# A graph network with a mixture of experts: the router's logits with the gate as standing operand, node numbers on three engines, and four groups

## The chip, the core and the metric

The kernel runs on one core of a Trainium2 chip. A core has TensorE (matrix products, into PSUM), VectorE, ScalarE and GpSimd, each with its own in-order queue, and SyncE, which only issues DMAs; they order their work by semaphores. The metric is the time of the device in microseconds, the median over runs.

## The reference

There are 6250 nodes with 256 features and 200000 edges sorted by destination. What is computed:

```
xn = layernorm(x)
x  = x + relu(GCN(xn)) + mix(xn)       # edges: gather, scale, sum by destination; mix: linear attention and MLP
h  = layernorm(x)                      # "x2" is this x
logits = h @ gate_w + gate_b           # 8 experts
idx = argmax(softmax(logits)); prb = its probability
pos = number of earlier nodes with the same idx
kept = pos < C                         # C = ceil(1.25 * 6250 / 8) = 977
y[n] = expert idx[n] (h[n]) * prb[n] * kept[n]     # 256 -> 1024 relu -> 256
out = x + nan_to_num(y)
```

An expert works on its kept nodes in the order of their numbers, at places 0 to 976. So the router has to turn the idx of each node into a list of node numbers by expert and place.

## The kernel before

Nodes lie in 49 blocks of 128 (a node is a partition of its block). Three stages follow each other: `prepare`, `aggregate_and_mix` (the edges, gathered by GpSimd's indirect DMAs, with the mix beside them) and `tail`. The tail is the router, some 95 us, and then the eight experts. Only the router and what touches its buffers is changed.

The router works in groups of blocks, given by RB (L64): 12, 12, 12, 8 and 5 blocks. All its order is written out by hand, in each engine's own program; within it:

- VectorE (loop at L1681 and behind) sums each block's x2 (L1456, tile acc), takes its statistics (L1461, stt), and after a group aggregates them (L1466, mvg). Between the blocks of a group it does the steps of the group before, at places that `steps` gives (of 24 gaps): `normal` (the root's input veps, the reciprocal inv, one Newton step, the columns of res for the feature table), `choose` (logits lg from PSUM, maximum, ex, candidate, one-hot oh), `counted`, `probability`, `assign`. `chain` lets an instruction raise the semaphore dv and `chained` waits for all that were chained so far, statistics too. In `assign` the place within the expert becomes a slot number; its upper part gives the one-hot one_hi (expert and row of 128, 64 columns), its lower 7 bits one_lo (128 columns), and two products with kept_lo and kept_hi put the node's number, in two parts, on one_hi (node_of, L1581 and L1584). In the second group four instructions low_w1 (L1613) for the first expert's weights stand between the blocks.
- TensorE takes blocks by pairs t: `turn` transposes a pair by four instructions (L1838, e_t), ScalarE copies it to xT_r (L1728), `logits` then multiplies with the pair's features as the standing operand and the 8 gate columns as the moving one (L1849): two products per block, each in two instructions for float32, so the logits come out with a node per partition. `places` counts the nodes before (L1863 to L1871), in the middle of the next group; `owners` (L1881) adds one_lo transposed times node_of over all blocks in p_map, after the last logits of the next group.
- ScalarE, per pair: copy, `scale` of two blocks (L1744, what goes to the feature table). Once a group a root (L1733), in front of the group's last copy, and an exponent (L1738); each of the two needs its own table, so a table load stands before each.
- SyncE sends for each group the feature rows (L1346) once its columns are there and the x2 rows (L1352); the load of w1 for the next expert (L1335) waits for the last low_w1.
- GpSimd makes constants at the start and then waits until slots_ok is 2 (slot_node is written, L1714) and all ten DMAs of the router have landed; then it gathers the first expert's rows (L1389).

## Time and profile before

| | us |
|---|---|
| median of 3 runs | 2598.12 (2594.09 to 2600.07) |
| the profiled execution's own time | 2596.97 |
| its span, first to last instruction | 2595.3 |
| TensorE busy, matrix instructions | 1927.2 |
| GpSimd busy | 1793.1 |
| VectorE busy | 1245.3 |
| ScalarE busy | 797.4 |
| mean granted TensorE clock | 0.874 |

The profile is of one execution. Its page has the busy time of each engine, the span in 40 slices, the chain of work that ended last and the costliest groups of instructions; the trace behind it can be asked for single stretches. PE is TensorE (PEld its weight loads), DVE is VectorE, ACT is ScalarE, POOL is GpSimd, SPq is SyncE's queue. A granted clock of 1.00 is 2.4 GHz, 0.50 is 1.2 GHz. L and a number is the line of the kernel.

### The profile page before, as it was taken

What the parts mean: (1) busy time and instruction counts of PE and PEld (TensorE: products, weight loads), DVE (VectorE), ACT (ScalarE), POOL (GpSimd) and SP (SyncE); (2) the same over time, 40 slices, a digit from 0 to 9 for tenths busy, and PEclk for the clock granted to TensorE, in tenths of its full rate; (3) what the DMA queues carried; (4) which work ended last, traced back from release to release, by engine and by line L of the source; (5) the groups of instructions that cost most, each with busy time, mean ns of one, the idle gap of its engine ahead of it and who ended that gap; (6) DMA issues with size and microseconds to landing.
All of it is one profiled execution on the core that took longest, in us unless ns stands there. A gap on an engine that the chain in (4) does not pass through costs nothing. (4 is left out here: it accounts for less than half of the span.)

```text
span 2595.3 us, 33207 instructions
## 1 busy us (share of the span) xinstructions
PE 1927.2 (74%) x8866; PEld 1534.0 (59%) x8866; DVE 1245.3 (48%) x3250; ACT 797.4 (31%) x1559; POOL 1793.1 (69%) x1908
## 2 busy tenths in 40 slices
PE   8588887666776766776777777766666676999997
PEld 6355555455555555655555555655444575888886
DVE  6334323344444453443544444443322385878886
ACT  5222222133333333332333333332000054444442
POOL 6577777777777777777777777777777602666665
PEclk9799999899888898888888888888877756999998
DMA  7433333333333333333333333333333444222220
GB/s 223 129 104 106 106 106 106 105 105 105 105 106 104 106 104 106 106 105 105 105 106 105 105 106 106 104 105 106 105 105 105 131 147 117 63 79 67 86 70 8
DMA packets 128069, 270.88 MB, mean 104 GB/s; under 512 B 33608, under 2 KB 71460, under 8 KB 127770
## 3 DMA queue, kind: packets, MB, share of 16 engines
q0 software_dynamic: 82992, 221.52, 29.9%
q1 hardware_dynamic: 44906, 47.32, 5.6%
q8 instruction: 77, 1.26, 0.2%
q14 instruction: 94, 0.77, 0.1%
HBM read 244.15 MB, written 27.35 MB: 105 GB/s over the span
## 5 line engine op out<-in xcount | busy, mean ns | idle before, releaser
L776 POOL DMA_INDIRECT ring<-node_rows,src_chunk x1563 | 1484.7, 950 | 493.1 <-issue 475.8
L800 PE MATMUL p_item<-ring,sel 128*128 x3512 | 1018.0, 434 | 536.8 <-SPq L757 534.3
L800 PEld LDWEIGHTS p_item<-ring,sel 128*128 128x128 f32 x3512 | 708.0, 214 | 774.7 <-issue 684.0
L1063 DVE TENSOR_TENSOR acc<-acc,p_item 128x256 f32 (+1 forms) x439 | 184.2, 419 | 826.7 <-PE p_item L800 822.4
L1045 DVE SCALAR_TENSOR_TENSOR sel<-dst_chunk,nbase,p_col 128x512 f32<-128x512 f32 x439 | 326.7, 744 | 57.1 <-issue 38.8
L1934 PE MATMUL e_y<-w2h,hTh 128*128 128x256 f32 x512 | 150.8, 295 | 3.6 <-DVE hTl L1643 3.6
L1389 POOL DMA_INDIRECT rows<-node_features,slot_row x64 | 72.3, 1130 | 114.5 <-DMA out_dram<-res 95.4
L1934 PE MATMUL e_y<-w2h,hTl 128*128 128x256 f32 x512 | 145.4, 284 | 0.0
L1934 PE MATMUL e_y<-w2l,hTh 128*128 128x256 f32 x512 | 145.3, 284 | 0.0
L957 ACT ACTIVATE x1T<-p_t,col_ln1b,col_ln1g 128x128 f32<-128x128 f32 x98 | 39.5, 453 | 343.9 <-PE p_t L833 343.9
L1141 DVE SCALAR_TENSOR_TENSOR kf<-p_q,ke 128x256 f32<-128x256 f32 x49 | 20.8, 425 | 203.7 <-ACT ke L940 203.7
L964 ACT ACTIVATE gT<-p_t,col_b 128x128 f32<-128x128 f32 x98 | 30.7, 364 | 266.8 <-PE p_t L841 266.8
L1921 PE MATMUL e_f<-bTh,w1h 128*128 128x490 f32 (+1 forms) x256 | 101.7, 397 | 11.8 <-ACT hbuf L1777 11.1
L1415 POOL TENSOR_TENSOR low<-low,big 128x256 f32<-128x256 f32 x64 | 51.8, 809 | 81.1 <-DVE big L1657 80.5
L1934 PEld LDWEIGHTS e_y<-w2h,hTh 128*128 128x128 f32 x512 | 98.6, 192 | 5.2 <-DVE hTl L1643 5.2
L1921 PE MATMUL e_f<-bTl,w1h 128*128 128x490 f32 (+1 forms) x256 | 100.3, 392 | 0.0
L1777 ACT ACTIVATE hbuf<-e_f,fb_sb 128x490 f32<-128x490 f32 (+1 forms) x128 | 80.0, 667 | 65.4 <-DVE hTl L1643 38.5
L1921 PE MATMUL e_f<-bTh,w1l 128*128 128x490 f32 (+1 forms) x256 | 99.4, 388 | 0.0
L1934 PEld LDWEIGHTS e_y<-w2l,hTh 128*128 128x128 f32 x512 | 98.8, 193 | 0.0
L1934 PEld LDWEIGHTS e_y<-w2h,hTl 128*128 128x128 f32 x512 | 98.5, 192 | 0.0
L869 PE MATMUL p_q<-wq_sb,xnT_m 128*128 128x512 f32 x196 | 97.5, 622 | 0.0
L1406 POOL DMA_INDIRECT out_dram<-oo,slot_node x64 | 79.1, 1236 | 26.5 <-DVE oo L1634 15.4
(257 smaller groups left out, 2921.9 us busy)
## 6 DMA issues: line engine op xcount, KB each, us to landing
ring<-node_rows,src_chunk POOLq DMA_INDIRECT x1563, 2.7
w1raw<-in_w SPq DMA_DIRECT2D x8, 1024.0 KB, 5.0
w2raw<-in_w SPq DMA_DIRECT2D x8, 1024.0 KB, 6.7
res<-in_x SPq DMA_DIRECT2D x7, 896.0 KB, 9.9
node_features<-res SPq DMA_DIRECT2D x3, 1554.0 KB, 7.5
out_dram<-res SPq DMA_DIRECT2D x3, 1536.0 KB, 10.6
node_rows<-acc SPq DMA_DIRECT2D x4, 1024.0 KB, 4.9
node_rows<-acc SPq DMA_DIRECT2D x3, 512.0 KB, 5.0
```

The costliest lines, as they stand in the source:

```text
L776: nc.gpsimd.indirect_dma_start(ring[:, c % RING // U, c % U, :], None, table, bass.IndirectOffsetOnAxis(src_chunk[:, c:c + 1], 0)).then_in ...
L800: mm = pe.matmul(p_item[bank(i)][:, 0:C], sel[:, i % SELR, u, :], rows[:, u, :], start=(u == 0), stop=(u == U - 1), skip_group_check=True)
L869: mm = pe.matmul(p_kv, xnT[:, a, :], wq_sb[:, a, C:3 * C], start=(a == 0), stop=(a == CH - 1))
L957: nc.scalar.activation(x1T[:, a, :], p_t[:, a, :], ACT.Identity, scale=g["cols"]["ln1g"][:, a:a + 1], bias=g["cols"]["ln1b"][:, a:a + 1]). ...
L1045: nc.vector.scalar_tensor_tensor(sel[:, i % SELR, :, :], dst.rearrange("p (u e) -> p u e", e=1).broadcast_to([P, U, P]), nbase[:, bass.ds( ...
L1063: nc.vector.tensor_tensor(a, a, p_item[bank(j)][:, 0:C], ALU.add).then_inc(added, 1)
L1389: nc.gpsimd.indirect_dma_start(rows[0:r, e % 2, t, :], None, feats, bass.IndirectOffsetOnAxis(slot_row[0:r, k:k + 1], 0)).then_inc((gather ...
L1406: nc.gpsimd.indirect_dma_start(out, bass.IndirectOffsetOnAxis(slot_node[0:r, k:k + 1], 0), oo[0:r, t % 2, :], None, bounds_check=N - 1, oo ...
L1415: nc.gpsimd.tensor_tensor(low[0:r, t % 2, :], low[0:r, t % 2, :], big[0:r, t % 2, :], ALU.add).then_inc(pool_st, 1)
L1777: nc.scalar.activation(hbuf[:, j % 2, h * NH[0]:h * NH[0] + NH[h]], p_f[(2 * j + h) % 4][:, 0:NH[h]], ACT.Relu, bias=fb1_sb[:, bass.ds(e, ...
L1921: mm = pe.matmul(p_f[c % 4][:, 0:NH[h]], w[:, a, j * P:(j + 1) * P], b[:, a, h * NH[0]:h * NH[0] + NH[h]], start=(q == 0), stop=(q == len( ...
L1934: mm = pe.matmul(p_y[t % 2][:, 0:C], h[:, j, t * P:(t + 1) * P], w[:, j, :], start=(q == 0), stop=(q == len(parts) - 1))
```

## The change

RB gives four groups of 14, 14, 14 and 7 blocks. The gate weights become the standing operand: one product for both blocks of a pair gives 8 partitions of up to 256 nodes, ScalarE copies these to lgT, and TensorE transposes them back to the bank that `choose` reads. node_of is no longer made by two products of VectorE: ScalarE makes the low part (a scaled copy with node_lo as the scale), GpSimd the high part, but VectorE for the last group. kept_lo and kept_hi are gone: the place is limited to RT * P - 1 = 1023, the last slot of an expert, which lies behind the 977 kept ones. The statistics raise bn_ok instead of dv. `owners` of a group comes one pair into the second group after it. The steps of VectorE stand at other places; low_w1 of the first expert stands behind the slots; ScalarE's root comes in front of the next group's first copy, in the last group in front of its last scale. one_lo and node_of share the memory of rows. The semaphores of the edges' dst rows are used again as arrived.

```diff
-RB = [0, 12, 24, 36, 44, NBLK]
-RGM = 12
+RB = [0, 14, 28, 42, NBLK]
+RGM = 14
...
GpSimd
-            nc.gpsimd.iota(e8[:], [[1, EXP]], EXP, 0, allow_small_or_imprecise_dtypes=True).then_inc(const3, 1)
+            nc.gpsimd.iota(e8[:], [[RT * P, EXP]], EXP * RT * P, 0, allow_small_or_imprecise_dtypes=True).then_inc(const3, 1)
...
+            pool.wait_ge(const3, 9)
+            for gi in range(NG - 1):
+                q, k = gi % 2, size(gi)
+                pool.wait_ge(one_hi_ok, gi + 1)
+                wait(pool, mapped, gi - 1)
+                nc.gpsimd.tensor_tensor(node_of[:, q, 0:k, 1, :], one_hi[:, q, 0:k, :],
+                                        node_hi[:, blocks(gi)].rearrange("p (b e) -> p b e", e=1)
+                                        .broadcast_to([P, k, NS]), ALU.mult).then_inc(high_node, 1)
             pool.wait_ge(slots_ok, 2)
             pool.wait_ge(dma_out, 16 * NOUT)
...
VectorE
-                chain(V.bn_stats(stt[:, gi % 2, b - RB[gi], :], acc[:, b, :]))
+                V.bn_stats(stt[:, gi % 2, b - RB[gi], :], acc[:, b, :]).then_inc(bn_ok, 1)
...
-                chained()
+                v.wait_ge(bn_ok, RB[gi + 1])
...
-                    chain(V.scalar_tensor_tensor(slot[:, 0:k], m2[:, 0:k], float(RT * P), place[:, 0:k], ALU.mult,
+                    chain(V.scalar_tensor_tensor(slot[:, 0:k], place[:, 0:k], float(RT * P - 1), m2[:, 0:k], ALU.min,
                                                  ALU.add))
-                    chain(V.scalar_tensor_tensor(kept_lo[:, 0:k], place[:, 0:k], float(CAP), node_lo[:, w], ALU.is_lt,
-                                                 ALU.mult))
-                    chain(V.scalar_tensor_tensor(kept_hi[:, 0:k], place[:, 0:k], float(CAP), node_hi[:, w], ALU.is_lt,
-                                                 ALU.mult))
...
-                    chain(V.tensor_tensor(one_hi[:, 0:k, :], counts(k, NS), over(slot_hi[:, 0:k], k, NS),
-                                          ALU.is_equal))
+                    V.tensor_tensor(one_hi[:, q, 0:k, :], counts(k, NS), over(slot_hi[:, 0:k], k, NS), ALU.is_equal
+                                    ).then_inc(one_hi_ok, 1)
                 if i == 5:
                     V.tensor_tensor(one_lo[:, q, 0:k, :], counts(k, P), over(slot_lo[:, 0:k], k, P), ALU.is_equal
-                                    ).then_inc(one_ok, 1)
-                if i == 6:
-                    chained()
-                    V.tensor_tensor(node_of[:, q, 0:k, 0, :], one_hi[:, 0:k, :], over(kept_lo[:, 0:k], k, NS),
-                                    ALU.mult).then_inc(one_ok, 1)
-                if i == 7:
-                    V.tensor_tensor(node_of[:, q, 0:k, 1, :], one_hi[:, 0:k, :], over(kept_hi[:, 0:k], k, NS),
-                                    ALU.mult).then_inc(one_ok, 1)
+                                    ).then_inc(one_lo_ok, 1)
+                    if gi == NG - 1:
+                        v.wait_ge(one_hi_ok, NG)
+                        V.tensor_tensor(node_of[:, q, 0:k, 1, :], one_hi[:, q, 0:k, :], over(node_hi[:, w], k, NS),
+                                        ALU.mult).then_inc(high_node, 1)
...
-                for i, k in enumerate((0, 5, 5, 6, 6, 7)):
+                for i, k in enumerate((0, 5, 6, 7, 8, 9)):
...
-                for i, k in enumerate((8, 8, 9, 9, 10, 10, 11, 11)):
+                for i, k in enumerate((10, 11, 12, 13, 13, 14, 15, 16)):
...
-                for i, k in enumerate((12, 13)):
+                for i, k in enumerate((17, 18)):
...
-                for i, k in enumerate((18, 19)):
+                for i, k in enumerate((20, 21)):
...
-                for i, k in enumerate((20, 20, 21, 21, 22, 22, 23, 23)):
+                for i, k in enumerate((22, 23, 24, 25, 26, 26)):
...
-                    if gi == 1 and u < PC:
-                        low_w1(0, u)
...
             v.wait_ge(dma_fb, 32)
+            for q in range(PC):
+                low_w1(0, q)
...
ScalarE
-                wait(s, l_ps, 2 * (t - XT) + 2)
+                wait(s, lt_ps, t - XT + 1)
...
+            def logits_out(t):
+                k = len(blocks_of(t)) * P
+                s.wait_ge(lt_ps, t + 1)
+                wait(s, l_ps, 2 * (t - 2) + 2)
+                nc.scalar.copy(lgT[:, t % 2, 0:k], p_lt[t % 2][0:EXP, 0:k]).then_inc(lt_sb, 1)
+
+            def node_low(gi):
+                q, k = gi % 2, size(gi)
+                s.wait_ge(one_hi_ok, gi + 1)
+                wait(s, mapped, gi - 1)
+                m = k - 1 if gi == NG - 1 else k
+                nc.scalar.activation(node_of[:, q, 0:m, 0, :], one_hi[:, q, 0:m, :], ACT.Copy, scale=node_lo[:, 0:1]
+                                     ).then_inc(low_node, 1)
...
             for gi in range(NG):
+                n = len(pairs(gi))
                 for i, t in enumerate(pairs(gi)):
-                    if i == len(pairs(gi)) - 1:
+                    if i == 0 and gi > 0:
+                        root(gi - 1)
+                    copy(t)
+                    if t > 0:
+                        logits_out(t - 1)
+                    if i == n - 1 and gi == NG - 1:
+                        node_low(gi - 1)
                         root(gi)
-                    copy(t)
-                    if i == 1 and gi > 0:
+                    if i == n // 3 and gi > 0:
                         exponent(gi - 1)
                     if t > 0:
                         scale(t - 1)
+                    if i == n - 1 and 0 < gi < NG - 1:
+                        node_low(gi - 1)
...
+            logits_out(-(-NBLK // 2) - 1)
             scale(-(-NBLK // 2) - 1)
             exponent(NG - 1)
+            node_low(NG - 1)
...
TensorE
-            def logits(gi, t):
+            def logits(t):
+                k = len(blocks_of(t))
                 t_.wait_ge(xT_ok, t + 1)
                 if t == 0:
                     t_.wait_ge(centred, CH)
+                wait(t_, lt_sb, t - 1)
+                for a in range(CH):
+                    mm = pe.matmul(p_lt[t % 2][0:EXP, 0:k * P], gate_sb[:, a, :], xT[:, t % XT, a:k * CH:CH, :],
+                                   start=(a == 0), stop=(a == CH - 1))
+                mm.then_inc(lt_ps, 1)
+
+            def logits_by_node(t):
+                gi = next(i for i in range(NG) if 2 * t < RB[i + 1])
+                t_.wait_ge(lt_sb, t + 1)
                 wait(t_, e_ok, gi - 1)
-                for b in blocks_of(t):
+                for i, b in enumerate(blocks_of(t)):
                     u = b - RB[gi]
-                    for a in range(CH):
-                        mm = pe.matmul(p_l[gi % 2][:, u * EXP:(u + 1) * EXP], xT[:, t % XT, b % 2 * CH + a, :],
-                                       gate_sb[:, a, :], start=(a == 0), stop=(a == CH - 1))
-                    mm.then_inc(l_ps, 1)
+                    pe.transpose(p_l[gi % 2][:, u * EXP:(u + 1) * EXP], lgT[:, t % 2, i * P:(i + 1) * P],
+                                 ident[0:EXP, 0:EXP]).then_inc(l_ps, 1)
...
             for gi in range(NG):
                 ts = list(pairs(gi))
                 for i, t in enumerate(ts):
+                    if t > 1:
+                        logits_by_node(t - 2)
+                    if gi > 0 and i == {7: 4, 4: 2}[len(ts)]:
+                        places(gi - 1)
                     turn(t)
                     if t == 0:
                         means()
-                    if i > 0:
-                        logits(gi, t - 1)
-                    if gi > 0 and i == {6: 3, 4: 1, 3: 0}[len(ts)]:
-                        places(gi - 1)
-                logits(gi, ts[-1])
-                if gi > 0:
-                    owners(gi - 1)
+                    if t > 0:
+                        logits(t - 1)
+                    if gi > 1 and i == 0:
+                        owners(gi - 2)
+            t = -(-NBLK // 2) - 1
+            logits_by_node(t - 1)
+            logits(t)
+            logits_by_node(t)
+            owners(NG - 2)
             places(NG - 1)
             owners(NG - 1)
```

## Rows read from the trace of the kernel before

**Rows 1.** The page: granted clock of TensorE in 40 slices of the span, in tenths.
```profile
PEclk9799999899888898888888888888877756999998
```
**Rows 2.** Stretches: length; busy PE, PEld, DVE, ACT, POOL; clock; DMA share, GB/s.
```profile
2148.00:2150.00 2.00, 0.97 (x5) 0.88 (x5) 1.97 (x4) 0.04 (x1) 0.00 (x0) 0.50 1.02 333
2024.50:2033.50 9.00, 6.19 (x14) 3.87 (x12) 1.92 (x4) 0.00 (x0) 6.78 (x8) 0.50 0.35 104
14.00:40.00 26.00, 25.76 (x143) 22.59 (x143) 23.19 (x107) 14.53 (x28) 15.95 (x17) 1.00 0.97 296
2068.80:2153.80 85.00, 65.95 (x370) 64.31 (x370) 71.45 (x271) 46.38 (x94) 0.00 (x0) 0.50 0.49 167
```
**Rows 3.** The chain of waits, router: start, us of the chain, what.
```profile
2067.45 0.34 DVE acc L1456
...
2067.84 0.66 PE e_t L1838 x4
2068.49 1.40 PE e_f L1849 x8
...
2087.37 0.95 PE e_t L1838 x4
2088.32 1.51 PE e_f L1849 x8
...
2089.91 0.47 PE e_f L1867 x11
...
2093.13 1.67 DVE one_lo_r L1577
2094.80 0.35 DVE stt L1461
...
2097.37 0.90 DVE mvg L1466 x12
...
2101.32 1.29 PE e_y L1881 x12
...
2156.31 5.70 DMA out_dram<-res
```
**Rows 4.** The timeline from the last logits to the first gathers.
```profile
2153.77 0.20 DVE L1501 TENSOR_TENSOR lg<-e_f,inv 128x40 f32<-128x40 f32 x1 [0.20 <-PE e_f L1849]
...
2160.80 0.23 DVE L1714 SCALAR_TENSOR_TENSOR slot_node<-node_f,gone 128x64 int32<-128x64 f32 x1
2162.78 0.97 POOL L1389 DMA_INDIRECT rows<-node_features,slot_row  x1 [95.39 <-DMA out_dram<-res]
...
2167.78 0.42 DVE L1608 TENSOR_TENSOR bTl<-e_t,bTh 128x256 fp32r<-128x256 f32 x1 [6.75 <-ACT bTh L1759]
```
**Rows 5.** The timeline of VectorE: w1l and a product of node_of.
```profile
2080.62 0.69 DVE L1613 TENSOR_TENSOR w1l<-w1raw,w1h 128x512 fp32r<-128x512 f32 x1
...
2095.18 0.96 DVE L1581 TENSOR_TENSOR node_of<-one_hi_r,kept_lo 128x768 bf16<-128x768 bf16 x1
```
**Rows 6.** The timeline of TensorE in the edge stage, at either clock.
```profile
2028.83 3.78 PE L800 MATMUL p_item<-ring,sel 128*128 x8 [1.91 <-SPq L757]
...
2053.85 1.99 PE L800 MATMUL p_item<-ring,sel 128*128 x8 [1.63 <-SPq L757]
```
**Rows 7.** The timeline of ScalarE, and TensorE's wait for it.
```profile
2098.82 0.57 ACT L1728 COPY xT_r<-e_t 128x512 f32<-128x512 f32 x1
...
2099.44 1.87 PE L1849 MATMUL e_f<-gate_sb,xT_r 128*128 128x8 f32 x8 [4.15 <-ACT xT_r L1728]
...
2145.85 0.89 ACT L1744 ACTIVATE res<-acc,dinv 128x256 f32<-128x256 f32 x2
2146.76 1.28 ACT L1733 ACT_TABLE_LOAD   x1
...
2152.31 0.35 ACT L1728 COPY xT_r<-e_t 128x256 f32<-128x256 f32 x1
```
**Rows 8.** Instructions of tile low: GpSimd's product in the expert stage, ns min/median/max.
```profile
L1415 POOL TENSOR_TENSOR low<-low,big x64: 714/748/1061, 2207.5 to 2585.9; 128x256 f32<-128x256 f32 x56, 81x256 f32<-81x256 f32 x8
```

60 lines of the change are left out of this document (35 added, 25 removed).

## The prediction
> **What bounds the kernel now.** I read the page first: in its 40 slices the granted clock dips to 5 and 6 tenths in two slices, the 33rd and 34th [rows 1], which is the router, the one stage that is changed. A window over its 85 us up to the last logits [rows 2] has no engine full: TensorE 66.0, VectorE 71.5, ScalarE 46.4, GpSimd 0. So the order of the work bounds it, and I read the chain of waits next [rows 3]. In a group it goes by TensorE: four transposes take 0.95 us of the chain and eight logit products 1.51, a pitch of 2.46 us for each pair of blocks. At a group's end it goes over to VectorE, whose one-hot and node-number products run for some 5 us while TensorE stands idle; then a square root, one copy on ScalarE, and TensorE goes on. From the first logits (2068.49) to the first VectorE step that reads the last ones (2153.77) are 85.3 us: 24 pitches are 59.0, owners and place counts about 8, and the idle time of TensorE the rest (19.0 us in that window). TensorE's clock is at its lower level, 1.2 GHz (0.50), all that time.
>
> After 2153.77 there is a fixed tail. The last rows of x2 are sent at 2156.31 and land 5.70 us later [rows 3], at 2162.01; slot_node is written at 2160.80, 1 us earlier; GpSimd's first row gather starts at 2162.78 [rows 4]. Behind it everything stays as it is (gathers, experts), so the change is worth what it moves 2162.78 by.
>
> **What it takes off VectorE.** Per group of 12 blocks two node_of products of 0.96 us each [rows 5], two small kept products, and stalls behind the statistics, for which I allow 1 us. The four pieces of w1l (0.68 us each, [rows 5]) leave the second group and now stand right after the slots: 2.7 us, hidden, since VectorE's next work waits for the gathered rows and came 6.8 us after slot_node [rows 4]; if that cover went, they would cost 2.7 us. Next comes group work per 14 blocks: 14 times a sum and a statistic at 0.67 us (the chain's acc 0.34 and stt 0.35, less what they overlap), 0.90 x 14/12 = 1.05 of aggregation, one_lo 1.67 x 14/12 = 1.95 [rows 3], one_hi with half its columns 1.0, small steps 4, stalls 1: about 18.2 us, or 2.6 us a pair. Were VectorE the bound, some 15 to 20 us would go. I must see whether it is.
>
> **What it does to TensorE.** Order per pair now: transpose back the logits of the pair before last, turn the new pair, then the wide logits of the pair before. Terms:
> 1. Turn: unchanged, 0.95 us.
> 2. Logits: each float32 product is two matrix instructions, and its 256 moving columns (two blocks) make one like those of the edge stage: p_item, 256 columns of float32. Eight of those take 1.99 us at 2.4 GHz and 3.78 us at 1.2 GHz from first start to last end [rows 6]. Four, with the latency of the last: 1.9 us at the lower level (half of 3.78), 1.07 at the upper (3 x 0.23 + 0.38). That the standing operand has 8 columns saves weight loads, not moving columns. Eight narrow ones took 1.51.
> 3. Hand-over: the transposes back are the very next TensorE instructions after these logits, and they wait until ScalarE has copied them out of PSUM. Nothing stands between, so latency and copy are bare: a copy of 256 elements is 0.35 us and the next TensorE instruction starts 0.05 us after a copy ends [rows 7]: 0.4 us. The copy of 256 elements on only 8 partitions is not in the trace; between nothing but its latency and 0.57 (the copy of a full pair) I take the 0.35 [rows 7].
> 4. Transposing back: two weight loads of 128 columns, one short product each: two of the eight in 1.51, 0.38 us; from 0.2 to 0.45.
> Sum at 1.2 GHz: 0.95 + 1.9 + 0.4 + 0.38 = 3.63 us a pair, against 2.46. At 2.4 GHz (turn 0.66 as at the router's start [rows 3], back 0.28): 2.4 us. The first is above VectorE's 2.6 and makes TensorE the bound; the second is not.
>
> **Which clock.** The trace has no wide product with 8 standing columns, so I bound it. Speaking for 1.2 GHz: the present router stays there for 85 us with TensorE 78% busy; in the edge stage a stretch of 9 us with 69% busy and eight wide float32 instructions per 5 us also stays at 0.50 [rows 2]. The new order has four such per 3.63 us, 47% of the time, plus the turns. Speaking against: the very first stage (14 to 40 us), transposes and wide products in the same manner but eight wide ones a pair and no bare hand-over, is at 1.00 throughout [rows 2]. I take 1.2 GHz. The fall to it comes with the router's first pairs, as now; 0.5 us off for them.
>
> **The sum.** First logits 2068.5. Logits of pair 23: + 23 x 3.63 = 83.5, - 0.5, + place counts of three groups (now 0.47 and a first product [rows 3], with 14 blocks 0.65) 2.0, + owners of two groups (1.29 x 14/12 = 1.5 each, of which 0.4 fills the hand-over) 2.2, - 0.45 for the single last block, + 1.3 for two group starts at which ScalarE (scale 0.9, low node numbers, table load 1.28, root, copy, [rows 7]) is 0.65 late. That is 2156.5. Then the last turn: these logits and their copy 2.3; in ScalarE's queue stand the low node numbers of group 2 (896 elements, about 0.95 us by the 0.57 for 512), the root with its table load (1.5), two scalings (0.9) and only then the copy out of the last logits (0.35): 3.7 us, all bare; the last transpose 0.5. VectorE reads the last logits at 2163.0, 9.2 us later than now. Spread of this part 2158 to 2166.
>
> Tail: from the last logits to the x2 DMA 2.54 us now [rows 3, 4]; ScalarE's scale and exponent table load stand the same way, 2.7. The two DMAs carry 7 blocks instead of 5, 0.51 MB more at the 333 GB/s of such stretches [rows 2], so 5.7 + 1.6 = 7.3. The slots are ready 7.4 us after 2163.0, so the DMA stays last: 2163.0 + 2.7 + 7.3 + 0.77 (from landing to gather now) = 2173.8. Against 2162.78 [rows 4]: + 11 us. The edits that cost nothing in this state: the node numbers on ScalarE (hidden but at the two places counted) and GpSimd, the limit of 1023, the statistics' semaphore, the later steps, all beside a TensorE that is behind; owners after the next group's first pair instead of at once: it ends TensorE's 4 us waits [rows 7], and those 19 us of idle are what pays for most of the longer pitch. The w1 load for expert 1 now starts some 3 us after the slots, beside the first gathers; 1 MB, up to 1 us, inside the bounds. The memory moved (one_lo and node_of on rows) is free, as rows is written after mapped.
>
> A rule against the change, outside the sum: the Trainium skill, SBUF — State Buffer, "Who interferes with whom", says that a VectorE instruction with two SBUF inputs and a GpSimd instruction that reads SBUF exclude each other for the whole instruction. By it GpSimd's product (896 elements; 0.75 us for 256 [rows 8], so about 2.6 us) could hold up VectorE's sums; with TensorE as the bound VectorE has about 1.7 us in hand before the last root, so the rule would add 0.9 us, by an estimate from row and rule together. No row of before has the two together in the router.
>
> **Rivals.**
> A. The clock rises for good near the start: pitch 2.4, then VectorE's 18.2 us a group. VectorE's last statistics come about 2136, lg at 2138, and the DMA of the 14-block group (3.6 MB, 10.8 us at 333 GB/s) is still running when the last 7 blocks are sent: landed 2146.6, gather 2147.4, - 15.4 us: 2583. It decides wherever the granted clock reaches 1.00 before the second group. For: the first stage of the kernel. Against: the numbers above. 12%.
> B. It rises late, for instance at the start of the third group, where logits and owners stand back to back for 3.4 us: nine pitches are about 1 us shorter each and the end 1 us: 2598, or down to 2590 if earlier. 20%.
> C. The hand-over is not bare (the sequencer or the copy hides it): pitch 3.04, 23 x 0.59 = 13.6 less: 2595. Against it is the plain order of the queue. 6%.
> D. The forecast, 62%.
> The change does what it says in all of them; VectorE does get lighter.
>
> **Numbers.** The profiled execution took 2596.97 us (span 2595.3), the median of three runs is 2598.12, 1.15 more; + 10.9 gives 2607.9 and 2609. I put 2608.5. A measurement of this kernel can tell about 0.2%, 5.2 us, from no change. D alone: 2602 to 2614 (lower and upper ends of terms 3 and 4, 23 x 0.25 either way, and 1 us for the DMA and the port). Left out of the range are A and a bit above: 2587 to 2614. Slower: D and none of the others, 0.62. Same: half of B, some of C, 0.13. Faster: A, the rest of B and C, 0.25.
>
> **What would show it.** In the changed profile: the granted clock over the router (0.50, else A or B); the pitch of turned pairs, 3.6 us; in the chain of waits the copy of the logits on ScalarE between TensorE's products and the transposes back, some 24 times; VectorE idle for over 20 us behind TensorE; the last root after the table load, with the logits' copy behind two scalings; the x2 DMA 7 to 8 us to landing and last before the gathers; w1l right after the slots without anyone waiting. Wrong would be: a wide logits group shorter than 1.7 us at 0.50, or first gathers before 2168.

## The result: 0.52% faster, where 0.4% slower was forecast

| | before | changed |
|---|---|---|
| median of 10 runs each, us | 2598.26 | 2583.95 |
| ratio, 95% interval | | 0.9948 (0.9938 to 0.9958) |
| the profiled execution, us (span) | 2596.97 (2595.3) | 2589.26 (2587.5) |
| router's first instruction to first gather of rows, us | 97.24 | 85.02 |
| first gather to the end of the span, us | 432.5 | 430.1 |

The profiled execution of the changed kernel is 5.3 us above its median, and its edge stage, which the change does not touch, ended late, at 2072.35 instead of 2065.54. So I compare from the router's first instruction (GpSimd's memset of ones_f) on. There the profiles differ by 12.2 us up to the first gather and by 2.4 behind it, together 14.6, and the medians by 14.3. The place of the gain is the router.

The page's clock line, which answers to [rows 1], has a 7, 9 and 7 in its 32nd to 34th slice, where before had 7, 5 and 6:
```profile
PEclk9799999798988888888888889888787797999998
```
The windows of the router in the changed kernel (answering to [rows 2]; columns as there) are from its start to the clock's rise, from there to the last logits, and the whole; then comes the stretch from the last logits to the first gather:
```profile
2072.40:2085.30 12.90, 10.30 (x38) 4.67 (x38) 12.49 (x51) 5.29 (x12) 1.73 (x9) 0.60 0.67 245
2085.30:2146.80 61.50, 42.75 (x288) 22.06 (x288) 45.57 (x184) 50.30 (x108) 10.13 (x3) 1.00 0.48 156
2072.35:2146.80 74.45, 53.05 (x324) 26.73 (x325) 58.07 (x235) 55.58 (x119) 11.91 (x12) 0.93 0.51 171
...
2146.80:2157.40 10.60, 2.95 (x30) 2.34 (x29) 8.32 (x27) 2.51 (x5) 0.03 (x1) 0.50 0.93 319
```
TensorE's clock is still at 1.00 when the router starts, falls to 0.50 2.6 us later, stays there for three pairs (10 us), and is then at 1.00 for 61 us. VectorE has 58.1 us of work in 74.5, where before it had 74.7 in 88.2.

The timeline of TensorE at the rise (start, us, then idle time and releaser in brackets) shows the pitch at both clocks:
```profile
2077.77 0.38 PE L1891 MATMUL e_f<-ident,lgT 8*128 8x8 f32 x2 [0.45 <-ACT lgT L1739]
2078.07 1.11 PE L1871 MATMUL e_t<-ident,acc 128*128 128x128 f32 x4
2079.12 1.88 PE L1881 MATMUL e_y<-xT_r,gate_sb 128*8 128x256 f32 x4
2081.45 0.38 PE L1891 MATMUL e_f<-ident,lgT 8*128 8x8 f32 x2 [0.45 <-ACT lgT L1739]
...
2085.12 0.30 PE L1891 MATMUL e_f<-ident,lgT 8*128 8x8 f32 x2 [0.45 <-ACT lgT L1739]
2085.36 0.66 PE L1871 MATMUL e_t<-ident,acc 128*128 128x128 f32 x4
2085.95 1.03 PE L1881 MATMUL e_y<-xT_r,gate_sb 128*8 128x256 f32 x4
```
From 2077.77 to 2081.45 are 3.68 us a pair (forecast for this clock: 3.63): transposes back, turn, four wide products at 1.88, and 0.45 of bare hand-over. The chain of waits has the pitch at 1.00, with ScalarE's copy in it, and then the tail up to the gather:
```profile
2092.57 0.28 PE e_f L1891 x2
2092.86 0.59 PE e_t L1871 x4
2093.44 0.97 PE e_f L1881 x4
2094.42 0.02 issue
2094.44 0.37 ACT lgT L1739
2094.81 0.04 issue
2094.85 0.29 PE e_f L1891 x2
...
2149.55 7.06 DMA out_dram<-res
...
2157.37 1.00 POOL rows L1393
```
2092.57 to 2094.85 are 2.28 us (forecast for this clock: 2.4). The x2 DMA takes 7.06 us (forecast 7.3; before 5.70, [rows 3]) and is still what the gather waits for. The waits of the engines in the router (total, times, longest):
```profile
PE e_f L1891 <- ACT lgT L1739: 16.7, 25, 3.6
DVE inv L1489 <- ACT sdg L1755: 12.3, 4, 8.5
...
PE e_t L1871 <- DVE acc L1468: 5.4, 6, 1.7
```
TensorE still waits 16.7 us for ScalarE, now 25 times for the copy of the logits. VectorE waits once 8.5 us for the first group's root. In a second profile of this kernel (e13 below), with the clock at 1.00 from the start, the same wait is 4.7 us: the 3.8 us between them are what the three pairs at 0.50 cost, since ScalarE's queue is late with the turns that it copies.

So the forecast's rival A happened (2583 against 2583.95). What I then had to find out was whether the wide logits with their clock brought the gain, or something else that the forecast had right or had missed.

### The profile page after: what moved, and what is told of

Its sections match the earlier page's. It is cut to its first block and busy times, and to the rows that moved or that the text cites. A ratio compares the mean times of both kernels' runs of the same rounds, so it can differ in the third digit from the quotient of the medians.

```text
span 2587.5 us, 33143 instructions
## 1 busy us (share of the span) xinstructions
PE 1909.0 (74%) x8818; PEld 1490.2 (58%) x8818; DVE 1232.7 (48%) x3205; ACT 805.1 (31%) x1585; POOL 1810.0 (70%) x1911
## 5 line engine op out<-in xcount | busy, mean ns | idle before, releaser
L1983 PEld LDWEIGHTS e_y<-w2h,hTh 128*128 128x128 f32 x512 | 97.8, 191 | 7.0 <-DVE hTl L1648 6.2
L1418 POOL DMA_INDIRECT out_dram<-oo,slot_node x64 | 81.1, 1267 | 26.6 <-DVE oo L1639 15.3
L1393 POOL DMA_INDIRECT rows<-node_features,slot_row x64 | 72.6, 1135 | 31.1 <-issue 19.1
```

The costliest lines, as they stand in the source:

```text
L1393: nc.gpsimd.indirect_dma_start(rows[0:r, e % 2, t, :], None, feats, bass.IndirectOffsetOnAxis(slot_row[0:r, k:k + 1], 0)).then_inc((gather ...
L1418: nc.gpsimd.indirect_dma_start(out, bass.IndirectOffsetOnAxis(slot_node[0:r, k:k + 1], 0), oo[0:r, t % 2, :], None, bounds_check=N - 1, oo ...
L1983: mm = pe.matmul(p_y[t % 2][:, 0:C], h[:, j, t * P:(t + 1) * P], w[:, j, :], start=(q == 0), stop=(q == len(parts) - 1))
```

## Experiments

All sixteen experiments and the two kernels are in one table. Ratios are to the kernel before in the same rounds. The two times count from the router's first instruction in the one profile; work is VectorE's busy time up to the last logits, clock the mean granted one of that stretch. "Narrow" is the changed kernel with the logits made as before; "covered" is the changed kernel with the copy of the logits beside other work of TensorE.

| | median us | ratio (95%) | to last logits | to gather | VectorE work | clock |
|---|---|---|---|---|---|---|
| before | 2598.26 | | 88.2 | 97.2 | 74.7 | 0.52 |
| changed | 2583.95 | 0.9948 (0.9938 to 0.9958) | 74.5 | 85.0 | 58.1 | 0.93 |
| e1 narrow | 2581.61 | 0.9935 (0.9914 to 0.9957) | 69.3 | 81.6 | 58.2 | 0.54 |
| e2 copied twice | 2599.75 | 0.9999 (0.9989 to 1.0008) | 90.3 | 100.1 | 58.3 | 0.80 |
| e3 wide alone | 2610.51 | 1.0046 (1.0028 to 1.0063) | 97.8 | 107.1 | 74.9 | 0.76 |
| e4 covered | 2578.97 | 0.9925 (0.9901 to 0.9950) | 65.6 | 76.1 | 57.8 | 0.97 |
| e5 order alone | 2598.41 | 0.9994 (0.9984 to 1.0004) | 87.5 | 96.5 | 74.5 | 0.52 |
| e6 narrow, old order | 2584.13 | 0.9932 (0.9914 to 0.9950) | 72.6 | 83.2 | 58.3 | 0.52 |
| e7 narrow, VectorE's products | 2585.55 | 0.9947 (0.9931 to 0.9964) | 76.3 | 86.0 | 63.8 | 0.50 |
| e8 narrow, old groups | 2587.17 | 0.9952 (0.9935 to 0.9968) | 80.3 | 89.2 | 61.8 | 0.50 |
| e9 copied three times | 2610.59 | 1.0030 (1.0018 to 1.0042) | 93.3 | 103.2 | 58.4 | 0.90 |
| e10 covered, late casts | 2582.14 | 0.9914 (0.9897 to 0.9930) | 69.4 | 80.0 | 58.0 | 0.87 |
| e11 narrow, late casts | 2587.25 | 0.9933 (0.9917 to 0.9950) | 71.4 | 83.6 | 58.2 | 0.52 |
| e12 narrow, statistics and w1l back | 2590.97 | 0.9951 (0.9935 to 0.9968) | 72.2 | 84.5 | 62.4 | 0.52 |
| e13 changed, again | 2579.77 | 0.9940 (0.9924 to 0.9956) | 70.7 | 81.1 | 58.1 | 0.98 |
| e14 narrow, again | 2581.33 | 0.9937 (0.9924 to 0.9950) | 71.7 | 82.4 | 58.3 | 0.50 |
| e15 covered, again | 2580.47 | 0.9926 (0.9913 to 0.9938) | 68.7 | 79.1 | 57.9 | 0.92 |
| e16 larger groups alone | 2587.82 | 0.9953 (0.9941 to 0.9966) | 77.8 | 89.1 | 68.2 | 0.55 |

One profile of a kernel against another of the same differs by 1 to 4 us in these stretches (81.1 against 85.0, 82.4 against 81.6, 79.1 against 76.1), so no difference below that is read here. A part of it is where the clock stands when the router begins: e14 began at 0.50, while e1 had 1.00 for its first 5 us and its last logits 2.4 us sooner.

### e1: narrow logits in the changed kernel
```
-                for a in range(CH):
-                    mm = pe.matmul(p_lt[t % 2][0:EXP, 0:k * P], gate_sb[:, a, :], xT[:, t % XT, a:k * CH:CH, :], ...
+                    for a in range(CH):
+                        mm = pe.matmul(p_l[gi % 2][:, u * EXP:(u + 1) * EXP], xT[:, t % XT, b % 2 * CH + a, :],
+                                       gate_sb[:, a, :], start=(a == 0), stop=(a == CH - 1))
...
-                        logits_by_node(t - 2)
-                        logits_out(t - 1)
```


> The changed kernel with one part undone: the logits are made as in the kernel before, block by block with xT as the standing operand, so there is no hand-over over ScalarE and nothing is transposed back; groups, node numbers on ScalarE and GpSimd, limit of 1023 and owners' place stay as changed. Measure: the time from the router's first VectorE instruction to the first gather of rows, 97.2 us in the profile before and 85.0 in the changed one. Theory W (the wide logits bring the gain, since with them the clock rises): the clock stays at 0.50, the pitch goes back to 2.46 us and the interval to about 96 us, time as before. Rival V (the lighter VectorE and the later owners bring it, the wide logits only pay for themselves by the clock that they raise): the clock stays at 0.50 as well, but TensorE needs only 25 x 2.46 = 61.5 us and some 9 for places and owners, without its idle time of before, so the interval is 84 to 87 us and the time within 3 us of the changed kernel's. If the clock rises here too, the transposes back and the wide form had nothing to do with it.

It took 81.6 us and was 0.65% faster than before, with the clock at 0.50 from 5 us after the start on. Theory W fell, and V held, even below its 84 us. The wide logits are not needed for the gain. The window of the second profile of this kernel (e14), up to the last logits:
```profile
2067.20:2138.90 71.70, 68.00 (x382) 67.48 (x383) 58.26 (x236) 47.80 (x94) 11.90 (x12) 0.50 0.53 179
```
TensorE is busy 68.0 of 71.7 us there, 95%, at 0.50.

### e2 and e9: the logits copied out twice, three times
```
                 nc.scalar.copy(lgT[...], p_lt[t % 2][0:EXP, 0:k]).then_inc(lt_sb, 1)
+                s.wait_ge(lt_sb, 2 * t + 1)
+                nc.scalar.copy(lgT[...], p_lt[t % 2][0:EXP, 0:k]).then_inc(lt_sb, 1)
...
-                t_.wait_ge(lt_sb, t + 1)
+                t_.wait_ge(lt_sb, 2 * t + 2)
```


> The changed kernel with one piece of work added: ScalarE copies each pair's logits out twice, one after the other, before TensorE may transpose them back: 0.36 us and a latency more of bare hand-over per pair, nothing else. Theory T (the clock rises because TensorE does enough between hand-overs, and at 3.68 us a pair it was near the edge): with about 4.1 us a pair at 1.2 GHz the clock stays at 0.50 through the router, 24 pitches are 24 x (4.1 - 2.3) = 43 us longer, the interval from the router's start to the first gather goes from 85 to about 125 us, and the kernel is some 1.0 to 1.5% slower than the kernel before. Rival (the clock rises in any case once wide logits are there): 1.00 from the third or fourth pair on, pitch 2.7, the interval about 92 us, and the kernel still faster than before.

Neither: 100.1 us. The clock rose 17.8 us after the router's start, stayed for 41 us and then went up and down (0.80 in the mean). TensorE's timeline at the rise shows the pitch at 1.2 GHz, 4.07 us, and 2.97 at 2.4 (the next one is 2.68):
```profile
2081.59 0.38 PE L1893 MATMUL e_f<-ident,lgT 8*128 8x8 f32 x2 [0.84 <-ACT lgT L1741]
...
2085.66 0.29 PE L1893 MATMUL e_f<-ident,lgT 8*128 8x8 f32 x2 [0.85 <-ACT lgT L1741]
...
2088.63 0.28 PE L1893 MATMUL e_f<-ident,lgT 8*128 8x8 f32 x2 [1.14 <-ACT lgT L1741]
```
The second copy costs 0.39 us a pair (4.07 less 3.68; at 2.4 GHz 2.68 less 2.28), so the hand-over is bare as forecast. Over 25 pairs 0.4 us are 10 us, and the kernel loses 15.8 to the last logits, its whole gain. The rest is not taken apart; it goes together with the clock, which was at 0.50 for longer at the start and again for 10 us in the middle.

The same with a third copy:

> The changed kernel with the logits copied out three times, each copy after the one before, so that TensorE's bare hand-over is 0.36 + 2 x 0.42 us: what the forecast's sum is worth where the clock is the one that it assumed. With two copies the pitch was 4.07 us at 0.50, 2.7 to 3.0 at 1.00, and the clock changed between the two. Theory S (the sum was right, the clock wrong): the clock stays at 0.50 from the third pair on, the pitch is 4.5 us, and from the router's start to the first gather are 108 us (97.2 + 11.0 of the forecast) + 23 x 0.84 = 127 us, within 3. Rival (at 0.50 VectorE or ScalarE would have bound the time in another way, or the idle time at the group ends would have come back): 5 us or more off that, either way; if the clock still rises in places, less by 1.3 us for each pair at 1.00.

It took 103.2 us, not 127, and was 0.30% slower than before: with still more idle time in TensorE (39 us against 29 in e2) the clock was at 1.00 for most of the stretch. Windows of the router in e2 and in e9:
```profile
2067.10:2157.40 90.30, 61.25 (x324) 30.20 (x325) 58.26 (x235) 64.78 (x144) 11.90 (x12) 0.80 0.44 148
```
```profile
2072.37:2165.60 93.23, 54.24 (x324) 27.16 (x325) 58.38 (x235) 73.50 (x169) 11.91 (x12) 0.90 0.44 141
```
My idea that the changed kernel had been near an edge, which a longer hand-over would put it below, fell. And the state that my sum assumed, wide logits at 0.50 to the end, never came, so its total is untested; only its pitch was seen.

### e3: wide logits alone in the kernel before
```
-                logits(gi, ts[-1])
+                logits_by_node(ts[-2])
+                logits(ts[-1])
+                logits_by_node(ts[-1])
```
(with the wide logits, logits_out and logits_by_node of the change; the rest as before)

> The kernel before with one part of the change alone: the gate's weights stand and the logits of a pair are four wide products, copied out by ScalarE and transposed back; groups of 12, node numbers all on VectorE and owners straight after a group's last logits stay as before (the lists of arrival semaphores are shared as in the change, which moves no work). Here two hand-overs are bare at each group's end. Theory T (the clock rises with the wide products as in the changed kernel): pitch 2.3 to 2.5 us at 1.00, a turn earlier or later in clock after each idle stretch at a group's end; the interval from router start to the first gather 94 to 100 us, time within 0.2% of before: wide logits alone give nothing. Rival (the forecast's clock, 0.50): pitch 3.65, 25 x 1.2 = 30 us more, the interval about 127 us, slower by 1.1%.

It was 0.46% slower and took 107.1 us, with the clock at 0.76 in the mean: neither the 94 to 100 us of theory T nor the 127 of the rival. It is the only part of the change that I tried alone and that costs. TensorE's largest wait in it:
```profile
PE e_f L1871 <- ACT lgT L1738: 31.0, 22, 6.0
```
It is 31.0 us in 22 pieces, and the longest, four of 3.7 to 6.0 us, stand at the group ends, behind the root and the last copy; the clock was at 0.50 after them.

### e4: the hand-over covered
```
-                    if t > 1:
-                        logits_by_node(t - 2)
                     if gi > 0 and i == {7: 4, 4: 2}[len(ts)]:
                         places(gi - 1)
                     turn(t)
+                    if t > 1 and not early:
+                        logits_by_node(t - 2)
```
(early is the last group's second pair, which keeps the old order)

> The changed kernel with the transposes back moved behind the next pair's turn, so that the copy on ScalarE runs beside four transposes (in the last group's second pair the order stays as it is). Theory H (TensorE's pitch with its bare hand-over sets the end): the pitch falls from 3.68 to about 3.25 us at 1.2 GHz and from 2.29 to about 1.9 at 2.4 GHz, the clock rises one or two pairs earlier, VectorE's 2.6 us a pair becomes the bound, the last logits come 3 to 6 us earlier, and the interval from router start to first gather is 79 to 82 us. Rival (VectorE or ScalarE is the bound at the upper clock already, TensorE only waits elsewhere): 84 to 86 us, no difference that can be measured.

It took 76.1 us and was 0.75% faster than before, more than theory H said. In this kernel the transposes back follow the turn without idle time (timeline of TensorE):
```profile
2091.09 0.66 PE L1871 MATMUL e_t<-ident,acc 128*128 128x128 f32 x4 [0.37 <-DVE acc L1468]
2091.68 0.28 PE L1891 MATMUL e_f<-ident,lgT 8*128 8x8 f32 x2
2091.89 1.03 PE L1881 MATMUL e_y<-xT_r,gate_sb 128*8 128x256 f32 x4
```
and what the turn waits for is VectorE's sum. To compare groups I take the stretch from the first logits step of VectorE (lg, L1513) to the second one, in which it sums 14 blocks in these kernels. It is 18.31 us here, where the changed kernel has 19.63 (e13). The window of this stretch, and VectorE's wait at its end:
```profile
2088.72:2107.03 18.31, 14.47 (x97) 7.75 (x96) 16.53 (x69) 15.23 (x33) 3.33 (x1) 0.91 0.60 202
```
```profile
2107.03 0.28 DVE L1513 TENSOR_TENSOR lg<-e_f,inv 128x112 f32<-128x112 f32 x1 [1.75 <-PE e_f L1891]
```
VectorE has 16.5 us of work in it and waits 1.75 us, for the logits.

### e5 and e6: the order alone, and the order undone
```
                 for i, t in enumerate(pairs(gi)):
-                    if i == len(pairs(gi)) - 1:
-                        root(gi)
+                    if i == 0 and gi > 0:
+                        root(gi - 1)
                     copy(t)
```
(and on TensorE the next group's first turn ahead of the last logits and the owners)

> The kernel before (narrow logits, groups of 12, node numbers on VectorE) with the order of the change alone: ScalarE takes a group's square root ahead of the next group's first copy instead of ahead of the group's own last copy, and TensorE turns the next group's first pair before it makes the last logits and the owners. Measure: router start to first gather, 97.2 us before, 81.6 us in the changed kernel with narrow logits; both at clock 0.50. Theory O (the 16.7 us that TensorE stood in four waits for ScalarE's last copy of a group, itself behind the root, are the gain): 83 to 87 us, most of the 15.6 us between the two. Rival V (VectorE sets a group's end anyway, at about 12 x 0.67 + small steps + two node-number products, so TensorE's wait only moves): 92 to 96 us.

It took 96.5 us and shows no difference in time: theory O fell. The wait of TensorE did not go, it moved. Kernel before, then e5, TensorE's waits in the router:
```profile
PE e_f L1849 <- ACT xT_r L1728: 16.7, 4, 4.6
PE e_t L1838 <- DVE acc L1456: 4.1, 4, 1.7
```
```profile
PE e_t L1840 <- DVE acc L1456: 16.3, 9, 4.2
```
and what ScalarE itself waited for at the four roots of the kernel before:
```profile
ACT sdg L1733 <- DVE veps L1474: 18.6, 4, 5.0
```
The 16.7 us behind ScalarE's copy, which my forecast read as the order's fault, are 16.3 us behind VectorE's sums as soon as the order is another. VectorE was late both times: ScalarE stood 18.6 us in four waits for veps, the root's input, which VectorE makes. The first stretch from one logits step to the next, with 12 blocks, in the kernel before and in e5:
```profile
2081.55:2101.90 20.35, 16.20 (x92) 15.88 (x91) 17.85 (x67) 11.07 (x22) 0.00 (x0) 0.50 0.46 156
```
```profile
2086.45:2105.89 19.44, 15.21 (x85) 14.93 (x85) 17.85 (x68) 11.29 (x22) 0.00 (x0) 0.50 0.49 164
```
and VectorE's one large wait in that stretch of the kernel before:
```profile
DVE cur L1554 <- PE e_f L1867: 1.8, 1, 1.8
```
Neither engine is full, at 16.2 and 17.9 of 20.35 us, but VectorE's work with its one large wait, 1.8 us for the place counts, is 19.7 of it. The 0.9 us by which e5 is shorter here don't reach the last logits (87.5 against 88.2).

> The changed kernel with narrow logits (81.6 us from router start to first gather) and the order of before: root ahead of a group's last copy, last logits and owners at the group's own end. VectorE stays relieved (node numbers on ScalarE and GpSimd, no kept products, statistics on their own semaphore), groups of 14. Theory O: TensorE waits again at three or four group ends, 3 to 4 us each, and the interval goes back by 9 to 14 us, to 91 to 95. Rival V (relief of VectorE is what counts): at most 4 us, 82 to 86, since VectorE reaches the group's end sooner.

It took 83.2 us against 81.6 and 82.4, as rival V has it: 1 to 2 us, and 0.9932 against 0.9935 and 0.9937 in time: nothing that I can tell.

### e7, e8, e12 and e16: the parts of VectorE's relief
e7, all products on VectorE:
```
+                    V.tensor_tensor(node_of[:, q, 0:k, 0, :], one_hi[:, q, 0:k, :], over(node_lo[:, w], k, NS), ...
+                    V.tensor_tensor(node_of[:, q, 0:k, 1, :], one_hi[:, q, 0:k, :], over(node_hi[:, w], k, NS), ...
```


> The changed kernel with narrow logits, with all node-number products on VectorE (for a group of 14 about 1.1 us each, two per group where there were none, one more in the last): 7 x 1.1 = 7.7 us more of VectorE. Theory O (TensorE is the bound with narrow logits, VectorE has some 0.1 us a pair less to do than TensorE): half of it shows at the group ends, 2 to 5 us: 84 to 87 us. Rival V (the relief is the gain): all 7.7 us, 89 us. A third: nothing, within 1 us of 81.6, since ScalarE's and GpSimd's parts are late themselves (TensorE waited 1.6 us for GpSimd's).

It took 86.0 us, inside theory O's 84 to 87: 3.7 to 4.4 us more for 5.6 us more of VectorE's work. So two thirds to four fifths of the added work show, though TensorE is nearly full in the narrow kernel.

e8, the groups:
```
-RB = [0, 14, 28, 42, NBLK]
-RGM = 14
+RB = [0, 12, 24, 36, 44, NBLK]
+RGM = 12
```
(the steps of VectorE keep their 28 gaps)

> The changed kernel with narrow logits, with the groups of before (12, 12, 12, 8, 5) instead of (14, 14, 14, 7). Theory O: a group's end costs TensorE about 0.5 to 1 us and ScalarE two table loads, so one more end gives + 1 to 2 us, while the last group has 5 blocks instead of 7 and its DMA lands sooner (8.86 us with 7 blocks, 5.70 before with 5): the two pay for each other, interval 79 to 84 us. Rival (fewer, larger groups are a part of the gain of their own): 85 us or more.

It took 89.2 us, 6.8 to 7.5 more: the rival held. It is the largest single step, though VectorE has only 3.6 us more of work. VectorE's logits steps in e8 show why:
```profile
2085.20 0.26 DVE L1513 TENSOR_TENSOR lg<-e_f,inv 128x96 f32<-128x96 f32 x1 [0.42 <-PE e_f L1874]
2102.66 0.26 DVE L1513 TENSOR_TENSOR lg<-e_f,inv 128x96 f32<-128x96 f32 x1
2121.42 0.26 DVE L1513 TENSOR_TENSOR lg<-e_f,inv 128x96 f32<-128x96 f32 x1 [0.75 <-PE e_f L1874]
2136.04 0.22 DVE L1513 TENSOR_TENSOR lg<-e_f,inv 128x64 f32<-128x64 f32 x1 [1.75 <-PE e_f L1874]
2147.98 0.19 DVE L1513 TENSOR_TENSOR lg<-e_f,inv 128x40 f32<-128x40 f32 x1
```
The stretches between them are 17.46, 18.76, 14.62 and 11.94 us, and VectorE sums 12, 10, 7 and 3 blocks in them. In e14 they are 20.00, 19.25 and 12.49 us with 14, 11 and 4 blocks. Three blocks still take 11.94 us: most of a stretch is what a group costs once (small steps, the waits for root, exponent and place counts), and e8 pays it five times instead of four.

e12, statistics and w1's low parts:
```
-                V.bn_stats(...).then_inc(bn_ok, 1)
+                chain(V.bn_stats(...))
...
+                    if gi == 1 and u < PC:
+                        low_w1(0, u)
```


> The changed kernel with narrow logits, with the two small edits undone that are left of VectorE's relief: the statistics on VectorE's common semaphore again, so that each wait for the last step also waits for them, and the four low parts of w1 (0.68 us each) in the second group instead of after the slots. The undone parts so far gave 1.6 (order), 4.4 (node-number products) and 7.6 us (groups) of the 15.6 between before and this kernel, so 2.0 are left if they add up. Theory: VectorE bounds the second group, and 4 x 0.68 = 2.7 us less what fits into its waits, plus 0.5 us a group for the semaphore: 83.5 to 86 us. Rival (the four have no meaning of their own and the sum only closes by noise): 81 to 82.5 us.

It took 84.5 us, inside the theory's range, but the last logits came 72.2 us after the start, as in e14 (71.7; e1 had 69.3), and against e14 the rest of the difference is a slower landing of x2 (8.86 against 7.21 us). The ratio is 0.9951 against 0.9935 and 0.9937, with intervals that overlap. Inconclusive: between 0 and 4 us.

e16, the counterpart from the other side:

> Narrow logits, the order of before, all node-number products on VectorE, statistics on the common semaphore, w1's low parts in the second group: of the change only groups of 14, 14, 14, 7, later steps, and places limited to 1023 (no kept products) remain. Undone one at a time the parts gave 1.6 (order), 4.4 (products), 7.6 (groups), 2.9 us (statistics and w1's low parts) of 15.6. Theory S (they add up): 97.2 - 7.6 = 89 to 91 us from router start to first gather, about 0.3% faster than before. Rival J (TensorE's waits for the root in the old order hide each other's gains unless VectorE is light): 93 to 97, within 0.1% of before.

It took 89.1 us and was 0.47% faster than before: theory S. Of the changed kernel's gain the larger groups, with the later steps and without the kept products, bring most by themselves. The first stretch between two logits steps, with 14 blocks:
```profile
2088.12:2110.28 22.16, 19.37 (x110) 19.06 (x110) 19.46 (x71) 12.47 (x25) 0.00 (x0) 0.50 0.50 167
```
That is 1.58 us a block against 1.70 (20.35 / 12); over 49 blocks 5.5 us. The last logits came 10.4 us sooner (77.8 against 88.2); what is left of that lies at the end, where a group is missing: behind its third logits step the kernel before has two more stretches, of 16.68 and 14.54 us, e16 behind the same step one, of 16.02. The gather came 8.1 us sooner, since the last x2 rows take longer to land (7.78 against 5.70 us).

### e10 and e11: ScalarE's casts out of the first group
```
-                    if gi == 0 and i in (3, 4):
-                        high_w1(0, 2 * i - 6)
-                        high_w1(0, 2 * i - 5)
...
+            for q in range(PC):
+                high_w1(0, q)
```


> The kernel with the covered hand-over (76.1 us from router start to first gather), with ScalarE's four casts of expert 0's w1 (0.56 us each) moved from the first group to after the last router step of ScalarE. Theory A (ScalarE is on the path in the first group: VectorE waited there for the root, which stood behind scalings and casts): VectorE starts the second group's normal step up to 2 us sooner, 74 to 75 us. Rival (VectorE's own load per block, 0.67 us twice a pair and the group's steps, sets the end): 76 us, within 0.5. If the casts come late for VectorE's w1l or the first expert products, it shows behind the gather: more than 431 us from there to the end.

> The same move of the four casts in the changed kernel with narrow logits (81.6 us, clock at 0.50). Theory A: TensorE is ahead of VectorE at no group's end by more than 1 us, so the sooner root gives 0 to 1 us: 80.6 to 81.6. Rival: ScalarE holds VectorE here as well, 79 to 80 us.

They took 80.0 us against 76.1 and 79.1, and 83.6 against 81.6 and 82.4: longer than either expectation allowed, by no more than two profiles of one kernel differ. Theory A fell in e10, and e11 shows no gain either: these profiles show no cost of the casts in the first group. Behind the gather e10 has 432.3 us, more than the 431 named above, but within the 427 to 434 of all profiles. By the ratio e10 is the lowest of all, 0.9914, but its interval overlaps those of e4 and e15, so this stays open.

### e13, e14 and e15: the three forms of the logits in the same rounds

> The changed kernel itself, for a comparison with the next three on one chip. Its clock in the router is one question: the first profile had 0.50 up to the third pair and 1.00 for the following 61 us. Expected by theory W (wide products bring the clock up each time): 1.00 over most of the router again, 84 to 87 us from router start to first gather. Rival (it was near an edge and came up by chance): 0.50 for a good part, 90 us or more. Ratio to before 0.994 to 0.996.

> The changed kernel with narrow logits again, beside the changed kernel in the same rounds. Theory N (the whole gain is VectorE's relief with the larger groups, the wide logits cost some us even at 1.00): 2 to 5 us faster than the changed kernel, interval from router start to first gather 81 to 84. Rival E (equal): within 1 us. Rival W (the wide logits bring something): slower than the changed kernel.

> The changed kernel with the transposes back behind the next pair's turn, again, in the same rounds. If the bare hand-over is what the wide logits cost: 4 to 8 us faster than the changed kernel and 1 to 4 us faster than the one with narrow logits, interval 76 to 80. Rival (VectorE bounds all three): the same as the narrow one within 1 us.

Medians 2579.77, 2581.33 and 2580.47: the three can't be told apart in time (0.9940, 0.9937, 0.9926). The changed kernel had its clock at 1.00 from the router's start to 2 us before the last logits this time and needed 81.1 us to the gather, below the 84 to 87 that I expected; in its own first profile, 85.0, the clock had fallen for the first pairs. Between the changed kernel and the narrow one rival E (equal) is nearest, though their medians are 1.6 us apart and the ratios order them the other way; for the covered one its ratio is the lowest of the three without being apart from them. The windows of the first stretch between two logits steps, with 14 blocks, in the changed and the narrow kernel, and in e2:
```profile
2087.37:2107.00 19.63, 14.87 (x102) 7.75 (x102) 16.73 (x69) 16.37 (x34) 3.33 (x1) 1.00 0.56 189
```
```profile
2087.15:2107.15 20.00, 19.87 (x115) 19.77 (x115) 16.74 (x69) 13.50 (x26) 3.33 (x1) 0.50 0.56 185
```
```profile
2094.37:2116.77 22.40, 14.82 (x104) 7.82 (x104) 16.73 (x69) 18.91 (x42) 3.33 (x1) 1.00 0.50 166
```
VectorE's work is the same in all, 16.7 us. What differs is how long it waits:

| | first stretch, us (blocks) | VectorE's work | its waits | a block | second stretch, us (blocks) |
|---|---|---|---|---|---|
| before | 20.35 (12) | 17.9 | 1.8 place counts | 1.70 | 20.65 (10) |
| narrow, old groups, e8 | 17.46 (12) | 14.9 | 1.6 place counts, 0.8 exponent | 1.46 | 18.76 (10) |
| larger groups alone, e16 | 22.16 (14) | 19.5 | 1.3 place counts, 1.1 exponent | 1.58 | 21.70 (11) |
| narrow, e14 | 20.00 (14) | 16.7 | 1.4 place counts, 1.3 root, 0.4 exponent | 1.43 | 19.25 (11) |
| changed, e13 | 19.63 (14) | 16.7 | 1.4 place counts, 1.3 root, 0.2 exponent | 1.40 | 18.62 (11) |
| covered, e4 | 18.31 (14) | 16.5 | 1.75 logits | 1.31 | 16.51 (11) |
| covered, e15 | 18.49 (14) | 16.5 | 1.9 logits | 1.32 | 17.86 (11) |
| e2 | 22.40 (14) | 16.7 | 2.5 root, 1.8 place counts, 1.4 exponent | 1.60 | 25.01 (11) |

The second stretch reaches into the next, smaller group, so it has fewer blocks. An engine's work and its waits always add up to about the stretch; what the table shows is that VectorE's work is 75 to 90% of each, and that the rest is a few round trips to ScalarE and TensorE. In the narrow kernel TensorE is full too, 19.87 of 20.00 us, at 0.50; in the changed one it has 14.9 us of work at 1.00 and stands 4.0 for the copies. So the wide logits win 0.4 to 0.6 us a stretch there, which no time shows, and 1.4 to 2.7 with the hand-over covered.

## Why the prediction was wrong, step by step

**What bounds the kernel: half wrong.** "The order of the work bounds it" rested on no engine being full and on TensorE's idle time at the group ends. e5 took the order away and left the time. What counts is VectorE's work, 74.7 us of 88.2, with its waits for exponent and place counts: 5.6 us less of that work is worth 3.7 to 4.4 us (e7), and one group less 6.8 to 7.5 (e8). A queue that waits for ScalarE, which itself waits for VectorE's variance, looks like ScalarE's or the order's fault in the list of waits.

**What it takes off VectorE: right in kind.** The forecast was 18.2 us a group (its own terms add up to 18.4); with 14 blocks it measured 19.63 (e13), of which 16.7 are work and 2.9 waits, where I had 17.2 and 1. Its work up to the last logits fell by 16.6 us. I saw this gain, but took it for one that only counts if VectorE is the bound, and put the case in which it would be at 12%.

**The four terms on TensorE: right.** The pitch was 3.68 us against 3.63 at 1.2 GHz, 2.28 against 2.4 at 2.4; wide logits 1.88 (1.9) and 1.03 (1.07); the copy of 8 partitions 0.37 (0.35); the hand-over bare 25 times. Rival C is refuted: e2 added 0.39 us to it and got it back in the pitch. (C took 0.59 us a pair off, more than the whole hand-over, which the forecast itself had at 0.4.)

**"I take 1.2 GHz": the step that failed.** In the changed kernel the clock was 0.93 in the mean up to the last logits, and behind the first three pairs the pitch was 2.28 us instead of 3.63. In eight profiles with wide logits (changed, e2, e3, e4, e9, e10, e13, e15) the clock was at 1.00 for most of the router, in nine with narrow ones (before, e1, e5 to e8, e11, e12, e14) at 0.50 but for its first microseconds, and in e16 so too, but for 3.4 us more at 1.00 later on. My reasons for 0.50 compared shares of busy time (78% and 69% at 0.50). In the runs that share does not tell the two levels apart: TensorE was busy 95% of e14's stretch at 0.50, and 58% of e9's at 0.90. The one row with the same kind of work, transposes and wide float32 products [rows 2, the stretch of 14 to 40 us], stood at 1.00; I named it and set it aside for its eight products and its missing hand-over. What the clock follows the runs don't settle, nor why it stayed at 1.00 at the router's start in e13 and fell for three pairs in the first profile.

**The sum.** With pitch 3.63 it put the last logits 9.2 us later than before; measured from the router's start they came 13.7 us earlier. Rival A, which differs only in the clock, had them 15.8 us earlier and ended at 2583 for 2583.95. Of its working, the last logits at 72.5 us after the router's start lie between the two profiles (74.5 and 70.7). From there to the gather it had 9.4 us, and 10.5 were measured. That it met the time so closely is in part luck: the narrow kernel, at 0.50 and without A's condition, is as fast (e14).

**The tail: right.** The DMA was last before the gather and took 7.06 us (7.3), and from its landing to the gather were 0.76 (0.77). w1's low parts stand right after the slots and nobody waits for them:
```profile
2154.39 0.22 DVE L1717 SCALAR_TENSOR_TENSOR slot_node<-node_f,gone 128x64 int32<-128x64 f32 x1
2154.53 2.49 DVE L1618 TENSOR_TENSOR w1l<-w1raw,w1h 128x512 fp32r<-128x512 f32 x4
```
They end at 2157.02; the first expert product starts at 2170.97.

**The last root behind the table load, the logits' copy behind two scalings.** They are there, but beside VectorE's own work, so the 3.7 bare microseconds of the forecast did not show as such.

**Owners after the next group's first pair: worth nothing here.** I let it pay for most of the longer pitch (19 us of idle time). e5 and e6, which move it together with the root, put the two at 0 to 2 us.

**GpSimd's product: held up by VectorE.** In the changed kernel it took 3.33 to 3.40 us for 896 elements, where the estimate was 2.6. VectorE's one_lo, which reads two operands in SBUF, GpSimd's product, and in the last group veps:
```profile
2106.35 2.02 DVE L1585 TENSOR_TENSOR one_lo_r<-col,slot_lo 128x1792 bf16<-128x1792 f32 x1
2106.59 3.33 POOL L1402 TENSOR_TENSOR node_of<-one_hi_r,node_hi 128x896 bf16<-128x896 bf16 x1 [32.38 <-DVE one_hi_r L1582]
...
2141.75 2.02 DVE L1585 TENSOR_TENSOR one_lo_r<-col,slot_lo 128x1792 bf16<-128x1792 f32 x1
2141.91 3.40 POOL L1402 TENSOR_TENSOR node_of<-one_hi_r,node_hi 128x896 bf16<-128x896 bf16 x1 [12.93 <-DVE one_hi_r L1582]
...
2144.75 0.58 DVE L1486 SCALAR_TENSOR_TENSOR veps<-deg,mvg 128x7 f32<-128x7 f32 x1
```
and the same instruction veps in e7, which has no product on GpSimd:
```profile
L1479 DVE SCALAR_TENSOR_TENSOR veps<-deg,mvg x4: 167/168/168, 2078.4 to 2141.7; 128x14 f32<-128x14 f32 x3, 128x7 f32<-128x7 f32 x1
```
By the rule of the Trainium skill, SBUF — State Buffer, "Who interferes with whom", one of the two would have had to wait for the other. The trace agrees: one_lo, which began first, took 2.02 us with GpSimd's product and without it (e7), and the product ended 1.54 to 1.56 us behind one_lo's end in every group and every kernel that has it, whether it had begun 0.16 or 0.24 us behind one_lo's start. For 768 and 512 elements (e8) it ended 1.33 and 0.90 us behind. So some 1.8 us of each 3.4 were waiting, and the product itself took about 1.55. In turn veps, with two operands in SBUF, was issued in the last group while the product still ran: it took 0.58 us instead of 0.17 and ended as the product did. That is 0.4 us in front of the last root, where the forecast had 0.9 by the same rule. In the narrow kernels TensorE's owners also waited 1.6 us for GpSimd's product of the third group (e1, e14).

**Where the gain is.** From before to the narrow kernel (e1, e14) it is 14.9 to 15.6 us up to the gather. The larger groups with the steps that came with them are 8.1 of it added first (e16) and 6.8 to 7.5 taken away last (e8); the products on ScalarE and GpSimd about 4 (e7); the order 0 to 2 (e5, e6); statistics and w1's low parts 0 to 3 (e12). From the narrow to the changed kernel it is nothing that a time shows (e13 against e14): the wide logits take TensorE from 19.9 us of work for 14 blocks to 14.9 by the clock that comes up with them, and give 4.0 back in bare hand-overs. Alone, with VectorE's load of before and the hand-overs bare at the group ends too, they cost 0.46% (e3). What is not settled: the 2.4 us behind the first gather (the other profiles have 427 to 434 us there, changed or not, so it may be nothing).

The best kernels are the covered ones, 0.75% and 0.74% faster than before (e4, e15) and 0.86% with the late casts (e10), against 0.52 to 0.60% for the changed one. In the rounds that had both (e13, e15) their intervals overlap, so which of them is the fastest is not shown.

## What to carry to other kernels

When an engine waits at a group's end, follow the chain on to what the releaser itself waited for, and add up for each engine its work and its large waits between two such ends: here VectorE's made up most of the group, and changing only the order moved the same 16 us of TensorE's wait from one line to another. What a group costs once (small steps, root and exponent round trips) is best saved by fewer groups: three blocks took 11.9 us, fourteen 20.0 (e8, e14). For a clock that can be at either of two levels, look for the row with the same kind of instructions, not for one with the same busy share, and when the two levels give results of opposite sign, keep both near even.
